# Token sums as a 129th column of a Gram product, and router logits by 32x32 transposes on VectorE

## Time and profile before

| | |
|---|---|
| median of 3 runs | 2330.44 us (2330.02 to 2330.62) |
| profiled execution | 2332.27 us |
| its span in the trace | 2330.5 us |
| TensorE busy | 2307.9 us, 99% |
| VectorE busy | 1701.6 us, 73% |
| ScalarE busy | 1162.4 us, 50% |
| GpSimd busy | 425.2 us, 18% |
| batch period, steady state | 142.80 us |

### The profile page before, as it was taken

The page is one execution under the profiler, slowest core; times in us unless marked ns, Lnnn a source line. Parts: engine busy times, 40 slices in busy tenths (PEclk is TensorE's granted clock), DMA queues, the critical chain, the costliest instruction groups (busy, mean ns, idle before and its releaser), DMA issues.

```text
span 2330.5 us, 35473 instructions
## 1 busy us (share of the span) xinstructions
PE 2307.9 (99%) x12414; PEld 1930.6 (83%) x12414; DVE 1701.6 (73%) x3016; ACT 1162.4 (50%) x1928; POOL 425.2 (18%) x353
## 2 busy tenths in 40 slices
PE   8999999999999999999999999999999999999998
PEld 7878888888888888888888888888888888888787
DVE  7977676867778677787777877768777777867643
ACT  5354554555454454645446454554454545454553
POOL 0111202121021211212112021220212102122200
PEclk9999999999999999999999999999999999999999
DMA  9266546576574765757656576675757657464342
GB/s 328 80 190 182 166 142 202 146 218 180 184 194 139 223 175 193 188 130 259 151 193 188 139 254 145 197 197 140 242 134 221 177 171 208 142 199 127 105 115 88
DMA packets 133138, 411.01 MB, mean 176 GB/s; under 512 B 29538, under 2 KB 32738, under 8 KB 122850
## 3 DMA queue, kind: packets, MB, share of 16 engines
q1 hardware_dynamic: 96722, 368.31, 48.9%
q0 software_dynamic: 16896, 33.56, 9.4%
q10 hardware_dynamic: 19344, 6.88, 1.4%
HBM read 381.90 MB, written 26.79 MB: 175 GB/s over the span
## 4 chain that ended last, share of the span: by engine, by line
PE 95%; DVE 2%; ACT 1%; issue 1%; DMA 1%; POOL 0%; SPq 0%; POOLq 0%; DVEq 0%; ACTq 0%
PE acc L1659 29%; PE m L1402 14%; PE h_ps L1635 10%; PE h_ps L1637 10%; PE h_ps L1636 10%; PE m L1432 7%; PE m L1512 2%; PE m L1590 2%; PE m L1495 2%; PE m L1494 2%; PE m L1493 2%; PE m L1616 1%; PE acc L1402 1%; PE m L1470 1%; PE m L1443 1%
## 5 line engine op out<-in xcount | busy, mean ns | idle before, releaser
L742 ACT ACTIVATE hid<-h_ps,b 128x512 f32<-128x512 f32 x252 | 173.6, 689 | 549.9 <-PE h_ps L1637 549.2
L1402 PE MATMUL m<-xT_hi,wq 128*128 128x512 f32 x1320 | 409.3, 391 | 1.8 <-DVE xT_lo L1361 1.8
L1659 PE MATMUL acc<-we_hi,h_hi 128*128 128x512 f32 x1008 | 401.1, 398 | 1.5 <-DVE h_lo L1238 1.5
L1635 PE MATMUL h_ps<-x2T_hi,we_hi 128*128 128x512 f32 x1008 | 399.1, 396 | 2.3 <-DVE x2T_lo L1222 2.3
L1659 PE MATMUL acc<-we_hi,h_lo 128*128 128x512 f32 x1008 | 393.1, 390 | 0.0
L1659 PE MATMUL acc<-we_lo,h_hi 128*128 128x512 f32 x1008 | 393.0, 390 | 0.0
L1637 PE MATMUL h_ps<-x2T_hi,we_lo 128*128 128x512 f32 x1008 | 392.8, 390 | 0.0
L1636 PE MATMUL h_ps<-x2T_lo,we_hi 128*128 128x512 f32 x1008 | 392.7, 390 | 0.0
L1238 DVE TENSOR_TENSOR h_lo<-hid,h_hi 128x512 fp32r<-128x512 f32 x252 | 204.3, 811 | 223.2 <-ACT h_hi L749 223.2
L1228 DVE TENSOR_TENSOR we_lo<-raw,we_hi 128x1024 fp32r<-128x1024 f32 x256 | 334.0, 1305 | 34.3 <-ACT we_hi L732 34.3
L662 ACT ACTIVATE e_f<-m,sb_qkv,scale 128x512 f32<-128x512 f32 x116 | 90.5, 780 | 478.3 <-PE m L1432 478.3
(11 more groups left out here) (301 smaller groups left out, 3583.8 us busy)
## 6 DMA issues: line engine op xcount, KB each, us to landing
raw<-in_w SPq DMA_DIRECT2D x256, 512.0 KB, 4.8
wq<-wq_scratch SPq DMA_DIRECT2D x168, 512.0 KB, 4.3
wp<-wp_scratch SPq DMA_DIRECT2D x84, 512.0 KB, 8.4
x<-in_x_tok SPq DMA_DIRECT2D x16, 1024.0 KB, 11.4
x<-in_b_proj POOLq DMA_DIRECT2D x16, 1024.0 KB, 12.3
ctx_T<-in_ctxT SPq DMA_DIRECT2D x16, 1024.0 KB, 7.2
x<-in_b POOLq DMA_DIRECT2D x16, 1024.0 KB, 11.8
ctx_tok<-in_ctx_tok SPq DMA_DIRECT2D x15, 1024.0 KB, 6.6
```

The source lines that it names most:

```text
L742: act.activation(hid[:, f % 2, :], up_bank(b, f)[:, :], ACT.Relu, bias=b1[:, b % 2, f:f + 1]).then_inc(h_done, 1)
L1402: pe.matmul(bank(a, j)[:, :], w[:, s, t, :], x_hi[:, t, :], start=(t == 0 and s == 0), stop=False)
L1635: pe.matmul(ps, we_hi[:, g % NW, js], x2T_hi[:, j, :], start=(j == 0), stop=False)
L1659: last = pe.matmul(acc[t][:, :], hx[:, f % 2, ts], wx[:, g % NW, C:], start=(f == 0 and n == 0), stop=(f == FC - 1 and n == 2))
```

## The change

- The context buffer gets a 129th column in each head's block, set to 1 once. In batches 2 to 15 (`WITH_SUMS`) the Gram matmuls are 129 columns wide; column 129 is the token sum of x1. Three heads fit in M2, the fourth goes to H_PS, so that `gram` waits for the hidden activation of up-projection 0 and up-projection 1 waits for the copy of the sums. `x_sums` and GpSimd's additions for it go.
- `scores_inner` moves from slot 34 to the end of slot 33 on VectorE and takes four instructions instead of two; ScalarE copies the sums in two small activations at slot 34.
- Everything that uses `ctx_tok` as y (`numerator`, `times_reciprocal`, `combine`, `low_block`, ...) reads or writes rows of 128 at steps of 129, and the context is loaded in runs of 128 elements.
- In batches 2 to 14 `means` and `logit_parts` go. Instead VectorE's `logits_by_block`, at slot 56 (h = 24), transposes `x_sum` in 32x32 blocks, sums, multiplies by the router's weights laid out for it (`wr_by_block`, one load more at the start), sums, transposes 32 columns and sums: six instructions, each waiting for the one before. The gather moves from slot 55 to the end of `mix` at slot 56 and the choice stays at 57. Waits for M2 that hung on the partial logits are replaced.

```diff
+WITH_SUMS = range(2, NB)
-GATHER = plan(55)
+LOGITS = plan(56)
+GATHER = plan(56)
...
-        ctx_tok = sb("ctx_tok", [P, TT, C])
-        y = ctx_tok
+        ctx_tok = sb("ctx_tok", [P, TT, XH, P + 1])
+        y = ctx_tok[:, :, :, 0:P]
...
+        def sums_copied(c):
+            return c + 1 if c < WITH_SUMS.start else 2 * (c + 1) - WITH_SUMS.start
+
+        def gram_out(c, h):
+            if c not in WITH_SUMS:
+                return by_head[:, h, :]
+            return M2[:, h * (P + 1):h * (P + 1) + P + 1] if h < XH - 1 else H_PS[:, 0:P + 1]
...
-                        sp.dma_start(context(a)[:, :, :], d["ctx_tok"][a]).then_inc(ctx_in, 16)
+                        sp.dma_start(context(a)[:, :, :, 0:P], d["ctx_tok"][a].rearrange("p t (h e) -> p t h e", h=XH)).then_inc(ctx_in, 16)
...
-                    if a > 0:
+                    if a > 0 and a not in WITH_SUMS:
                         tile_sum(a, xsum_done)
...
+                if (c := at(i, h, SCORES)) is not None and c in WITH_SUMS:
+                    act.wait_ge(sc_done, 12 * c + 2)
+                    act.wait_ge(sq_done, 3 * c - 1)
+                    act.activation(s_x[:, 0:XH - 1], M2[:, 0:(XH - 1) * (P + 1)].rearrange("p (h e) -> p h e", h=XH - 1)[:, :, P], ACT.Copy).then_inc(sx_done, 1)
+                    act.activation(s_x[:, XH - 1:XH], H_PS[:, P:P + 1], ACT.Copy).then_inc(sx_done, 1)
...
                 for v, wqv in enumerate((WQG, WQL)):
+                    if c in WITH_SUMS:
+                        some = XH - 1
+                        dve.tensor_tensor(s_a[:, v, 0:some, :], M2[:, 0:some * (P + 1)].rearrange("p (h e) -> p h e", h=some)[:, :, 0:P],
+                                          cols[:, wqv, 0:some].unsqueeze(2).broadcast_to([P, some, P]), ALU.mult)
+                        dve.tensor_scalar(s_a[:, v, some, :], H_PS[:, 0:P], cols[:, wqv, some:XH], None, ALU.mult).then_inc(sc_done, 1)
+                        continue
...
+            def logits_by_block(e):
+                n = 5 * (e - LOGITS_BY_DMA.start)
+                by_token = c_sb[:, :, :].rearrange("p h e -> p (h e)")
+                col_sums = junk_v[:, 1, 0:C // 32]
+                by_row, turned = junk_v[:, 0, 0:32], junk_v[:, 0, 64:96]
+                dve.wait_ge(x2sum_done, (TT - 1) * e)
+                if n > 0:
+                    dve.wait_ge(parts_in, 16 * (e - LOGITS_BY_DMA.start))
+                else:
+                    dve.wait_ge(route_mm, routed(e - 1) + 1)
+                dve.transpose(by_token, x_sum[:, :]).then_inc(lean_done, 1)
+                dve.wait_ge(lean_done, n + 1)
+                dve.reduce_sum(col_sums, by_token.rearrange("p (f i) -> p f i", i=32), AX.X).then_inc(lean_done, 1)
+                dve.wait_ge(lean_done, n + 2)
+                per_expert = by_expert[:, :].rearrange("p (s f) -> p s f", s=NE)
+                dve.scalar_tensor_tensor(per_expert, col_sums.unsqueeze(1).broadcast_to([P, NE, C // 32]), 1.0 / T, wr_by_block[:, :, :],
+                                         ALU.mult, ALU.mult).then_inc(lean_done, 1)
+                dve.wait_ge(lean_done, n + 3)
+                dve.reduce_sum(by_row[:, 0:NE], per_expert, AX.X).then_inc(lean_done, 1)
+                dve.wait_ge(lean_done, n + 4)
+                dve.transpose(turned, by_row).then_inc(lean_done, 1)
+                dve.wait_ge(lean_done, n + 5)
+                dve.reduce_sum(part_logits[:, 0:1], turned, AX.X).then_inc(part_done, 1)
...
-                if (c := at(i, h, MEAN)) is not None:
+                if (c := at(i, h, MEAN)) is not None and c not in LOGITS_BY_DMA:
                     logit_parts(c)
+                if (c := at(i, h, LOGITS)) is not None and c in LOGITS_BY_DMA:
+                    logits_by_block(c)
...
                     if (c := at(i, h, CHOOSE)) is not None and c in LOGITS_BY_DMA:
                         choose(c)
+                    if (c := at(i, h, GRAM)) is not None and c in WITH_SUMS:
+                        scores_inner(c)
...
                 if o == 2:
-                    pe.wait_ge(part_done, a)
+                    pe.wait_ge(res2_done, TT * a)
...
+                if c in WITH_SUMS:
+                    pe.wait_ge(made, MADE + 1)
+                    pe.wait_ge(h_done, FC * (c - 1) + 1)
+                wide = P + 1 if c in WITH_SUMS else P
                 for h in range(XH):
                     hs = slice(h * P, h * P + P)
                     for t in range(TT):
-                        last = pe.matmul(by_head[:, h, :], X[c % NX][:, t, hs], context(c)[:, t, hs], start=(t == 0), stop=(t == TT - 1))
+                        last = pe.matmul(gram_out(c, h), X[c % NX][:, t, hs], context(c)[:, t, h, 0:wide], start=(t == 0), stop=(t == TT - 1))
...
+                if f == 1 and b + 1 in WITH_SUMS:
+                    pe.wait_ge(sx_done, sums_copied(b + 1))
...
-                if (c := at(i, h, X_SUM)) is not None:
+                if (c := at(i, h, X_SUM)) is not None and c not in WITH_SUMS:
                     x_sums(c)
...
-                if (c := at(i, h, MEAN)) is not None:
+                if (c := at(i, h, MEAN)) is not None and c not in LOGITS_BY_DMA:
                     means(c)
```

More of the change, by code:

```diff
@@ L308, in ahead, with tiles, tiles_of_two, quarter_y @@
             return a == 1 and CC * j + t < AHEAD
+        def tiles(x):
+            return x.rearrange("p (t e) -> p t e", e=P)
+        def tiles_of_two(x):
+            return x.rearrange("p k (t e) -> p k t e", e=P)
         def numer(a):
-            return X[NX - 1] if a == 1 else y
+            return X[NX - 1][:, :, :].rearrange("p c (t e) -> p c t e", e=P) if a == 1 else y
+        def quarter_y(a, k, n):
+            return numer(a)[:, 2 * k:2 * k + 2, 2 * n:2 * n + 2, :]
+        def sums_copied(c):
[4 more added lines that the diff above has]
+            return M2[:, h * (P + 1):h * (P + 1) + P + 1] if h < XH - 1 else H_PS[:, 0:P + 1]
         def qk(a):
@@ L322, in context @@
         def context(c):
-            return X[NX - 1] if c == 1 else ctx_tok
+            return X[NX - 1][:, :, :].rearrange("p t (h e) -> p t h e", h=XH) if c == 1 else ctx_tok
         def staged(j):
@@ L532, in _ @@
             pool.wait_ge(made, MADE)
-            pool.wait_ge(consts_in, 16 * 3)
+            pool.memset(ctx_tok[:, :, :, P:P + 1], 1.0).then_inc(made, 1)
+            pool.wait_ge(consts_in, 16 * 4)
             def rstd_of(n, b):
@@ L580, in mix @@
                     if (due := upto(a - 1, 1, 1)) is not None:
-                        pool.wait_ge(mean_mm, due)
-                    if a > 0:
+                        pool.wait_ge(part_done, due)
+                    if a > 0 and a not in WITH_SUMS:
                         tile_sum(a, xsum_done)
@@ L604, in mix @@
                     pool.wait_ge(g_mm, c + 1)
-                    pool.wait_ge(xsum_done, (TT - 1) * c)
+                    if c not in WITH_SUMS:
+                        pool.wait_ge(xsum_done, (TT - 1) * c)
                     for t in range(TT):
@@ L684, in high_part @@
                 act.wait_ge(y_done, CC * a + cc + 1)
-                act.activation(y_hi(a)[:, cc, :], numer(a)[:, cc, :], ACT.Copy).then_inc(yhi_done, 1)
+                act.activation(tiles(y_hi(a)[:, cc, :]), numer(a)[:, cc, :, :], ACT.Copy).then_inc(yhi_done, 1)
             def high_block(a, b):
@@ L690, in high_block @@
                     act.wait_ge(y_done, CC * a + (2 if b == A11 else 4))
-                    raw_b = quarter(numer(a), *{A11: (0, 0), A12: (1, 0), A22: (1, 1)}[b])
+                    raw_b = quarter_y(a, *{A11: (0, 0), A12: (1, 0), A22: (1, 1)}[b])
                 else:
                     act.wait_ge(sum_done, 4 * k + {S3: 1, S1: 2, S2: 3, S4: 4}[b])
-                    raw_b = raw_sum(b)
-                act.activation(piece(a, b, 0), raw_b, ACT.Copy).then_inc(yhi_done, 1)
+                    raw_b = tiles_of_two(raw_sum(b))
+                act.activation(tiles_of_two(piece(a, b, 0)), raw_b, ACT.Copy).then_inc(yhi_done, 1)
             def prepare(i, h):
@@ L803, in mix @@
                     act.activation(const_b[:, :], M2[:, :], ACT.Copy).then_inc(kb_done, 1)
-                if (e := at(i, h, GATHER)) is not None and e in LOGITS_BY_DMA:
-                    act.wait_ge(part_done, e + 1)
-                    if e > LOGITS_BY_DMA.start:
-                        act.wait_ge(lsum_done, e - LOGITS_BY_DMA.start)
-                    act.dma_start(logit_row[0:1, :], part_logits[:, 0:1], allow_slow_non_contiguous=True).then_inc(parts_in, 16)
                 if (z := at(i, h, FFN + 44)) is not None:
@@ L874, in mix @@
                     normalise(0, a)
+                if (e := at(i, h, GATHER)) is not None and e in LOGITS_BY_DMA:
+                    act.wait_ge(part_done, e + 1)
+                    if e > LOGITS_BY_DMA.start:
+                        act.wait_ge(lsum_done, e - LOGITS_BY_DMA.start)
```

(10 more changed lines are left out.)

43 lines of the change are left out of this document (25 added, 18 removed).

## The result

| | before | after |
|---|---|---|
| median of 6 runs each | 2330.39 us (2329.93 to 2331.87) | 2317.82 us (2315.99 to 2319.13) |
| profiled execution, its span | 2332.27, 2330.5 us | 2315.99, 2314.4 us |
| TensorE, VectorE busy | 2307.9, 1701.6 us | 2294.4, 1704.2 us |
| batch period, steady state | 142.80 us | 141.88 us |

A forecast was written before the change was run, and what follows sets the result against it. TensorE, busy 99%, was taken to bound the kernel. Removed matmuls 15.6 us, less 0.4 for column 129 and 3.1 for product 2's wait, gave 12.1 us: 2318.3 us, own range 2315.3 to 2322.5, 8 in 10 2314.5 to 2326.5.

The forecast's parts named there:

- TensorE is the bound: Whole kernel: TensorE, busy 99% of the span, sets the time; what leaves its stream comes off unless new waits arise.
- `x_sums` removed, 0.59 us: TensorE's token sums of x1 go in batches 2 to 15: 0.59 us each, 8.3 us in all.
- means removed, 0.56 us: TensorE's means of x2 go in batches 2 to 14: 0.56 us each, 7.3 us in all.
- Column 129, 0.03 us: Gram product on TensorE: one column more adds 0.03 us per batch, 0.4 us over 14.
- the rival of slow passes: Gram product: operand steps of 516 B make its passes twice as long, about 2367 us; chance 0.03.
- Wait at product 2, 0.26 us: VectorE's 2.45 us logits chain delays A22's low part; TensorE's product 2 loses 0.26 us, 12 times, 3.1 us.
- Nothing later falls due first, `choose` as before: Behind the logits chain: product 3 keeps 0.5 us to spare; weight loads behind `choose` wait for VectorE's splits as before.
- Waits around the Gram product, nothing: Between Gram product and up-projection 1: sums ready 3.4 us ahead of need, covered by 5.5 us; cost nothing.
- GpSimd loses three additions a batch; it bounds nothing: GpSimd's additions for the x1 sums go; priced at nothing.
- DMA, nothing: Context load in 512 B runs, 2048 packets: estimated 3.5 us, about as long as now; cost nothing.
- The sum: Whole kernel: 15.6 - 0.4 - 3.1 = 12.1 us less, 2318.3 us, 0.5% faster; chance 0.58.

The follow-up runs named there:

- experiment 3: The whole change, but the six logits instructions stand behind S4 and A22's low part in the same slot: 2313.52 us, ratio 0.9933 to the kernel before.
- 1: Only the token sums by column 129 added to the kernel before; means and partial logits stay on TensorE and VectorE as before: 2322.01 us, ratio 0.9963.
- 2: Only the logits by VectorE in batches 2 to 14 added to the kernel before; token sums by `x_sums` as before: 2325.65 us, ratio 0.9983.
- Experiment 5: The kernel of experiment 3, with batch 15's fourth Gram head going to M0 instead of H_PS: 2313.7 us, ratio 0.993 to the kernel before.
- experiment 7: The kernel of experiment 3, with GpSimd still doing its three additions of x1's tiles, result unused: 2316.68 us, ratio 0.9943 to the kernel before.
- 9: The kernel of experiment 3 unaltered, run beside the unaltered change on the same chip: 2313.77 us, ratio 0.9936 to the kernel before.

## Why the prediction was right, step by step

- **TensorE is the bound**: right. Every part of the gain is matmuls gone or a wait of TensorE.
- **`x_sums` removed, 0.59 us; means removed, 0.56 us**: right, 1.14 for both in experiment 3, 0.56 and 0.58 apart in 1 and 2. It mattered to count from the matmul ahead of a group to the second one behind it: by the distance of the starts alone (0.39) the first would have been a third too small.
- **Column 129, 0.03 us**: 0.00; the Gram product takes 3.49 us with it and without. A mis-sized term of 0.4 us in all, and the rival of slow passes is dead.
- **Wait at product 2, 0.26 us**: the place, the releaser and the 12 times are right, the size is 0.22. The chain is 2.46 us for 2.45, but by errors that cancel: the two blocks of 512 columns and the small transpose take somewhat more than I had, the multiplication 0.29 instead of 0.346. The slack had grown by 0.05 us (2.40 in experiment 3 against 2.35). The resumption (0.05) and the slow first step (0.12) are as forecast.
- **Nothing later falls due first, `choose` as before**: right for the change. The addition ahead of product 6 ends at least 2.64 us before it in every batch. The term that was not worked out is how long the transfer of the logits takes; it decides in the late version (experiment 3).
- **Waits around the Gram product, nothing**: right for 13 of the 14 batches, wrong for the last. The prediction counted 5.5 us behind the product and did not ask what is ahead of it in batch 15, where no projection lies between up-projection 0 and the Gram product: 1.04 us, once. Experiment 5 takes this wait away and meets the one of product 6.
- **"GpSimd loses three additions a batch; it bounds nothing"**: wrong as a reason to price it at nothing. When they return, in experiment 7, the kernel loses 1.6 us in the last batch (190.11 against 188.50). That a stall vanishes with them, 1.36 of the 1.95 us behind Gram 15, was not in the forecast, and it more than pays for the missed wait.
- **DMA, nothing**: right in time. The context load lands in 6.3 us on the page of after, against 6.6, and in 6.2 to 7.6 in the experiments that have it in runs of 512 B; TensorE waits for it in none. The packets that I had counted are not to be seen (133278 in all against 133138), so that the estimate had the right end by a wrong way.
- **The sum**: 12.1 forecast, 12.3 and 12.6 by the medians. The steady part is as forecast; the close agreement of the total has some luck in it. By the terms as measured it would be 12.1 + 1.4 (the stall) - 1.0 (batch 15) + 0.5 (the wait is 0.04 shorter, 12 times) + 0.4 (the column) - 0.1 (both removals 1.14 for 1.15) = 13.3. The table without the late load has 13.1, the first profile of the change counted in the same way 13.15 - 0.9 = 12.25. The medians have 12.3 and 12.6. Two executions of one kernel thus differ by as much as is left to explain, and the runs of one kernel lie 3 us apart, with start-ups that differ by as much.

## What to carry to other kernels

When an edit puts a chain of dependent instructions on an engine with much idle time, its price is set by the next instruction on that engine that the bounding engine waits for: compare the chain with that slack to a tenth of a us, and look first for a place behind the waiter in the same slot. Here that was worth 2.6 us, but it moved the shortage on: the result's transfer then landed after its reader was due, and product 6, the next matmul to hang on that reader, was late in some batches. So follow the chain's result to its consumer too, and count the transfer between them. Check such a cover in the first and the last batches by themselves, since there the jobs of a neighbour that hide it are missing. And take work off a mostly idle engine if it shares something with a busy one: its operations can be the reason that a short instruction took three times as long. Whether that is worth anything is decided where the bounding engine waits, which was at one place here.

## What the runs showed of the hardware

- A VectorE transpose in 32x32 blocks of 128x512 float32 takes 0.70 to 0.71 us and a 512-column sum 0.69, both at the pace of a plain subtraction of that size (0.68). A transpose of 32 columns takes 0.21.
- A VectorE operation with two SBUF inputs that starts after a GpSimd operation of 2.3 us took 2.38 us instead of 0.69. The same in the steady period beside GpSimd's additions: the multiplication of `k_sum` took 1.77 us before and 0.69 after. It cost time only where TensorE was waiting for it.
- At product 2 TensorE resumes 0.05 us after VectorE's end, and its first 256-column step then takes 0.12 us more. At product 6 it is 0.15 and 0.07 (experiments 5 and 9).
- The same 0.5 KB transfer landed 2.6 to 3.4 us after its issue in batches 3 to 14 of the change, and 5.3 to 7.5 us where it was issued 1.2 us later in the slot. In batch 2 it took 7.0 to 7.2 us in both.
- A 129-column float32 pass with a moving operand at steps of 516 B takes what a 128-column one does (3.49 us for 32, from the first to the next matmul).
- Going from whole tiles to 32-column tiles costs 0.09 us; the first 512-column step behind a group of short passes takes 0.09 us more behind whole tiles and 0.11 behind 32-column tiles.
